# Moving the preparation of the batches from a stage of its own into the rows of the attention stage

## The chip, the cores and the metric

The kernel runs on one core of a Trainium2 chip. The core has five engines with a queue of instructions each: TensorE (PE), VectorE (DVE), ScalarE (ACT), GpSimd (POOL) and SyncE (SP, which here only issues DMAs). They run on their own and wait for each other through semaphores; every engine works its queue strictly in order. The metric is the device time of one execution in microseconds (us); the median of some runs is compared.

## The reference

A block over 16 batches of 512 positions of width 128. The input is normalised; what follows is relative-position attention with 16 heads of 8, a second small attention, and a mixture of experts. The change touches the first two lines and the attention.

```python
xn = layernorm(x)                                   # (16, 512, 128)
q, k, v = xn @ Wq.T + bq, xn @ Wk.T + bk, xn @ Wv.T + bv
idx = clip(pos[None, :] - pos[:, None], -20, 20) + 20
attn = softmax((q @ k.T + einsum("bhqd,qkd->bhqk", q, rel_k[idx])) / sqrt(8))
w = attn @ v + einsum("bhqk,qkd->bhqd", attn, rel_v[idx])
y = x + w @ Wo.T + bo + ffn(xn)
```

## The kernel before, in words

The program is a chain of four stages, each a block of its own between barriers: `prepare`, `attend`, `mix`, `experts`. Names of tiles carry the stage: `p_`, `a_`, `m_`, `e_`; `scr_` is scratch in device memory, through which the stages talk.

**prepare** goes over the 16 batches, two buffers of everything. For batch b it normalises x (statistics on DVE, the power on POOL, the scaling on DVE), transposes it (PE, bank `p_bank_xt`, read by ACT into `p_xnt`), and multiplies it by the three weights (`p_bank_q`, `_k`, `_v`). q, k and k less the left edge (`T[0..2]`, tiles `p_t`) are each split into three bf16 parts, high, middle and low (`p_sp`; the difference that is left is `p_rest`). The relative products (`p_bank_qr`, four query tiles of two halves each, 128x320) are q times the table of relative keys; one half is read by DVE (L201), the other by ACT (L305). POOL takes the products' first column out of them (`qr0`). Everything goes to `scr_parts`, `scr_qr`, `scr_v`, `scr_xn`; `scr_y` gets x + bo. All eight PSUM banks serve this stage.

**attend** goes over the batches again in unrolled rows, one row for a batch, and each row has 16 units u (four query tiles t of four units). A unit computes the scores of four blocks (bank `a_bank_s`, four banks, worked as two pairs):

- PE: scores of pair 0, the transposes of the probabilities of the unit before, j = 0 and 1, scores of pair 1, the products with V of three units before (`attended`, `a_bank_o`), the transposes j = 2 and 3. The scores of a pair may only start when ACT has emptied it in the unit before.
- DVE: for each pair the relative window is added (L815), the negated maximum taken (L846), and one transposed block copied out of the bank (L832, odd j).
- ACT: for each pair one transposed block copied (L899, even j), then two exponentials (L919).

The transposes share **two banks**, `a_bank_pt` 0 and 1. Every user of them is a job in the list `JOBS`, sorted by unit; job n has bank n mod 2, PE does the jobs in this order, and a job may start when the job before it in the same bank has been read. Besides the four `probs` jobs of each unit there are two `features` jobs at the end of every unit with u % 4 = 0 (first one read by ACT, L931, second by DVE, L868) and two `out` jobs at the end of unit 9. After u % 4 = 1 PE does `weigh` and DVE sums and a reciprocal; after u % 4 = 3 DVE does sums.

POOL makes the windows (`a_win`), the features and V with its bias. SP loads everything for the row after: the parts of q, k, kl in 18 DMAs that the list SPREAD hands out over the units (L566), the windows, v and y, and stores the probabilities of each unit.

Of the kernel before, what the change touches and what calls it, by code (L numbers as in the profile page):

```python
# [42 lines left out]
def prepare(nc, x, w, scr, ident_dram):  # L43

    with ExitStack() as ctx:
        def sb(name, shape, dt=F32):  # L50
            return ctx.enter_context(nc.sbuf_tensor("p_" + name, shape, dt))

        def ps(name):
            return ctx.enter_context(nc.psum_tensor("p_bank_" + name, [P, 512], F32))

        def sem(name):
            return ctx.enter_context(nc.semaphore("p_s_" + name))

        ident = sb("ident", [P, P])
        wq, wk, wv = sb("wq", [P, P]), sb("wk", [P, P]), sb("wv", [P, P])  # L60
        qk_bias = sb("qk_bias", [P, 4])
        bias_q = sb("bias_q", [P, 1])
        bias_kl = sb("bias_kl", [P, 1])
        rel = sb("rel", [P, H, FAR + 1])
        relx = sb("relx", [P, H, FAR])
        bo = sb("bo", [P, E])
        X = [sb(f"x{s}", [P, NT, E]) for s in range(2)]
        XN = [sb(f"xn{s}", [P, NT, E]) for s in range(2)]
        Y = [sb(f"y{s}", [P, NT, E]) for s in range(2)]
        stats = sb("stats", [P, NT, 6])  # L70
        mv = sb("mv", [P, NT, 2])
        pows = sb("pows", [P, 2])
        ones = sb("ones", [P, H])
        rstd = sb("rstd", [P, NT])
# [1748 lines left out]
```

## Time and profile before

| | us |
|---|---|
| three runs | 2536.8, 2535.61, 2541.07; median 2536.8 |
| profiled execution, its own time | 2541.16 |
| its span | 2539.2 |
| busy PE, DVE, ACT, POOL | 2166.0, 1971.7, 1574.5, 995.5 |
| first work of `attend` | 239.16 |
| first scores of `attend` | 284.35 |
| last exponential of `attend` ends about | 1624 |

The views list, for a stretch, a line or an instruction: how long an engine was busy, and how long it sat idle before an instruction and what ended that wait. A busy engine waits for nobody, an idle one shows who is late.

### The profile page before, as it was taken

How to read it: one execution, taken by the hardware profiler on the slowest of the kernel's cores; microseconds unless marked ns; L12 is line 12 of the kernel's file. 1: busy time of each engine (PE TensorE's matmuls, PEld its weight loads, DVE VectorE, ACT ScalarE, POOL GpSimd, SP SyncE). 2: the span in 40 equal slices, each digit the busy share in tenths (PEclk: the TensorE clock that was granted, in tenths of full speed). 3: DMA queues.
4: the chain of work that ended last, by engine and by line, in shares of the span. 5: the costliest groups of instructions: out<-in, count | busy, mean ns of one | idle time of the engine just before them, and what ended most of it. 6: DMA issues, size and time to landing. Idle time of an engine off the chain costs nothing. (4 is left out here: it accounts for less than half of the span.)

```text
span 2539.2 us, 78048 instructions
## 1 busy us (share of the span) xinstructions
PE 2166.0 (85%) x27816; PEld 1483.5 (58%) x27816; DVE 1971.7 (78%) x4345; ACT 1574.5 (62%) x3954; POOL 995.5 (39%) x1318
## 2 busy tenths in 40 slices
PE   5673488888888888888888888789999996999999
PEld 3442366666666666666666666546666554666665
DVE  5664399898989889888999999646776765787777
ACT  4442378787877777777878787546777662232222
POOL 5664245445554555455545554300000003333332
PEclk9877699999999999999999999879999998999999
DMA  6887255555554555545555554300101011011010
GB/s 192 268 256 224 81 111 123 110 115 111 125 113 110 117 119 113 116 105 124 111 115 118 118 119 88 65 18 26 37 25 37 25 33 60 29 30 32 25 37 17
DMA packets 572137, 241.21 MB, mean 95 GB/s; under 512 B 466374, under 2 KB 535750, under 8 KB 567238
## 3 DMA queue, kind: packets, MB, share of 16 engines
q1 hardware_dynamic: 571846, 237.28, 37.5%
q8 instruction: 189, 3.10, 0.5%
q14 instruction: 102, 0.84, 0.1%
HBM read 133.87 MB, written 103.29 MB: 93 GB/s over the span
## 5 line engine op out<-in xcount | busy, mean ns | idle before, releaser
L919 ACT ACTIVATE a_probs<-a_bank_s,a_neg_max 128x512 f32<-128x512 f32 x1024 | 694.0, 684 | 203.2 <-DVE a_neg_max L846 199.6
L846 DVE TENSOR_REDUCE a_neg_max<-a_bank_s 128x2 f32<-128x1024 f32 x512 | 626.9, 1224 | 55.7 <-DVE a_bank_s L815 1.4
L694 PE MATMUL a_bank_pt<-a_ident,a_probs 128*128 128x128 f32 x4096 | 590.9, 284 | 54.2 <-ACT a_feat_t L931 42.3
L694 PEld LDWEIGHTS a_bank_pt<-a_ident,a_probs 128*128 128x128 f32 x4096 | 443.1, 142 | 193.1 <-issue 68.8
L899 ACT ACTIVATE a_probs_t<-a_bank_pt 128x512 f32<-128x512 f32 x512 | 304.9, 596 | 146.9 <-PE a_bank_pt L694 144.8
L832 DVE COPY a_probs_t<-a_bank_pt 128x512 f32<-128x512 f32 x512 | 349.3, 682 | 27.5 <-PE a_bank_pt L694 22.1
L715 PE MATMUL a_bank_o<-a_probs_t,a_v 128*32 128x128 f32 x8192 | 285.9, 282 | 1.0
L682 PE MATMUL a_bank_s<-a_kl,a_q 48*32 48x204 bf16 (+14 forms) x3840 | 156.2, 273 | 128.7 <-DMA a_kl<-scr_parts 78.9
L1589 ACT ACTIVATE e_gate<-e_bank_g 128x512 f32<-128x512 f32 x144 | 85.9, 597 | 275.8 <-PE e_bank_g L1528 275.8
L715 PEld LDWEIGHTS a_bank_o<-a_probs_t,a_v 128*32 128x32 f32 x8192 | 215.0, 112 | 56.7 <-issue 33.8
L1005 POOL TENSOR_TENSOR a_win<-a_raw,a_band 128x1152 f32<-128x1152 f32 x64 | 168.6, 2634 | 126.8 <-DVE a_neg_max L846 69.6
L815 DVE TENSOR_TENSOR a_bank_s<-a_bank_s,a_win 128x144 f32<-128x144 f32 (+2 forms) x640 | 161.4, 270 | 57.9 <-PE a_bank_s L682 52.7
L1536 PEld LDWEIGHTS e_bank_y<-e_w,e_hid 128*128 128x128 f32 x1152 | 149.5, 192 | 96.6 <-issue 57.0
L1278 DVE TENSOR_REDUCE m_neg_max<-m_bank_s 128x2 f32<-128x1024 f32 x128 | 156.6, 1224 | 61.4 <-PE m_bank_s L1242 54.1
L919 ACT ACTIVATION_READ_ACCUMULATOR a_probs<-a_bank_s,a_neg_max 128x1 f32 x1024 | 203.2, 198 | 0.0
L682 PEld LDWEIGHTS a_bank_s<-a_kl,a_q 48*32 48x32 bf16 x3840 | 63.2, 89 | 219.1 <-issue 203.6
L1375 ACT ACTIVATE m_probs<-m_bank_s,m_neg_max 128x512 f32<-128x512 f32 x256 | 173.3, 682 | 13.4 <-DVE m_neg_max L1278 5.0
L1251 PEld LDWEIGHTS m_bank_pt<-m_ident,m_probs 128*128 128x128 f32 x1024 | 112.5, 143 | 99.7 <-issue 83.4
L1536 PE MATMUL e_bank_y<-e_w,e_hid 128*128 128x128 f32 x1152 | 156.0, 279 | 17.1 <-DVE e_hid L1698 17.1
L682 PE MATMUL a_bank_s<-a_k,a_q 48*32 48x512 bf16 (+15 forms) x4096 | 169.3, 291 | 0.0
L1341 POOL TENSOR_TENSOR m_rms<-m_rms,m_pows 128x4 f32<-128x4 f32 x16 | 16.1, 1007 | 371.3 <-DVE m_rms L1291 371.3
L1613 DVE SCALAR_TENSOR_TENSOR e_y<-e_bank_y,e_comb,e_y 128x128 f32<-128x128 f32 x512 | 143.8, 343 | 12.3
(166 smaller groups left out, 3576.3 us busy)
## 6 DMA issues: line engine op xcount, KB each, us to landing
scr_probs<-a_probs SPq DMA_DIRECT2D x512, 72.0 KB, 2.7
a_raw<-scr_qr SPq DMA_DIRECT2D x256, 96.0 KB
scr_qr<-p_qr SPq DMA_DIRECT2D x64, 320.0 KB, 2.9
a_feat<-scr_probs SPq DMA_DIRECT2D x256, 78.0 KB, 2.4
scr_parts<-p_sp SPq DMA_DIRECT2D x144, 128.0 KB, 2.9
a_left<-scr_probs SPq DMA_DIRECT2D x256, 64.0 KB, 2.4
a_q<-scr_parts SPq DMA_DIRECT2D x32, 192.0 KB
a_k<-scr_parts SPq DMA_DIRECT2D x32, 192.0 KB
```

The source lines that it names most:

```text
L682: ins = nc.tensor.matmul(b_s[g * QBLK:(g + 1) * QBLK, p, a:z], Q[s][par:par + ROWS, half, at:at + QBLK], keys[s][par:par + ROWS, half, a:z ...
L694: ins = nc.tensor.transpose(b_pt[bank_of(job)][:, 0, t * P:(t + 1) * P], probs[(u - 1) % 4][:, j, MAX_REL + t * P:MAX_REL + (t + 1) * P], ...
L715: ins = nc.tensor.matmul(out, V[s][:, V_SLOTS.index((edge, kt)), j, hh * 24:hh * 24 + 32], blocks[:, :, :, kt * P + j * QBLK:kt * P + (j + ...
L815: ins = nc.vector.tensor_tensor(near, near, bass.AP(own.tensor, own.offset, [own.ap[0], [step, n], [1, z - a]]), ALU.add)
L832: nc.vector.tensor_copy(probs_t[(u - 1) // 2 % 2][:, spot(u - 1, PLACES[j]), :], b_pt[bank_of(job)][:, 0, :]).then_inc(pt_ev[bank_of(job)], 1)
L846: nc.vector.tensor_reduce(neg_max[:, 2 * pair:2 * pair + 2], b_s[:, 2 * pair:2 * pair + 2, :], AX.X, ALU.max, negate=True).then_inc(max_ok, 1)
L899: nc.scalar.activation(probs_t[(u - 1) // 2 % 2][:, spot(u - 1, PLACES[j]), :], b_pt[bank_of(job)][:, 0, :], ACT.Copy).then_inc(pt_ev[bank ...
L919: nc.scalar.activation(probs[u % 4][:, j, MAX_REL:MAX_REL + S], b_s[:, j, :], ACT.Exp, bias=neg_max[:, j:j + 1], accum_out=sums[:, t, PLAC ...
L1005: nc.gpsimd.tensor_tensor(win[t % 2][:], over, band[:].rearrange("p (o h c) -> p o h c", o=1, h=1) .to_broadcast([P, NQB, NJ, WIN]), ALU.m ...
L1278: nc.vector.tensor_reduce(neg_max[:, 2 * pair:2 * pair + 2], b_s[:, 2 * pair:2 * pair + 2, :], AX.X, ALU.max, negate=True).then_inc(max_ok, 1)
L1375: nc.scalar.activation(probs[:, j, :], b_s[:, j, :], ACT.Exp, bias=neg_max[:, j:j + 1], accum_out=sums[s][:, u, j:j + 1]).then_inc(exp_ok, 1)
L1536: ins = nc.tensor.matmul(b_y[k][:, t * P:(t + 1) * P], hid[k][:, t * P:(t + 1) * P], w2[:, e, :], start=True, stop=True)
```

## The change

The stage `prepare` is gone; `attend` holds its work. Row b of the attention prepares batch b + 2 (LEAD = 2). Batch 0 is prepared ahead of everything, and batch 1 in a new row −1 (`lead`), which holds no attention. Rows 0 to 13 hold both kinds of work, rows 14 and 15 attention alone.

- The prepared batch's banks are 12 more jobs in the two banks `a_bank_pt`: the transposed x at the end of unit 3, q at 5, k at 6, v at 13, and two halves of a relative product at each of 10, 11, 14 and 15.
- ACT alone reads the relative products, 128x320 each, and with it takes their first column by an activation of 8 elements (`a_qr_first`), which POOL did. It also makes all the high and middle parts. DVE keeps the statistics (unit 0) and the reading of q (unit 5). POOL normalises x, and makes all differences and low parts.
- Each product of a relative half contracts over the 64 rows that hold its heads, not 128.
- k less the left edge is made from k in SBUF, no longer from the bank.
- v goes from the bank to the tile that POOL reads, without `scr_v`. x + bo is made by POOL in the row that ends the batch, from x loaded there, without the first pass through `scr_y`.
- SP has 19 issues more in a row with preparation (x, xn, nine parts, four of qr, four of the first columns), one less for v; the loads of q, k, kl begin at unit 3.

```diff
-def prepare(nc, x, w, scr, ident_dram):
...
+LEAD = 2
...
+PREP = [(3, "xt", 0), (5, "q", 0), (6, "k", 0), (13, "v", 0)] + [(u, "qr", n) for u in (10, 11, 14, 15) for n in range(2)]
+JOBS += PREP
 JOBS.sort(key=lambda job: job[0])
...
-        SPREAD = [1, 1, 2, 1, 1, 1, 2, 0, 1, 1, 2, 1, 2, 1, 1, 0]
+        SPREAD = [0, 0, 0, 2, 1, 1, 2, 2, 1, 1, 2, 1, 2, 2, 1, 0]
...
+            row(-1, 1, -1, lead=True)
             row(0, 0, 0, first=True)
...
+            for u in range(UNITS):
+                prep(-LEAD, u)
+            prep_rest(0)
+            sp.wait_ge(out_qr, 16 * NT)
+            sp.wait_ge(out_0, 16 * NQB)
+            sp.wait_ge(out_sp, PART_STORES)
             load_left(0, 0)
             load_win(0, 0)
             load_qk(0, 0, STACK)
...
+                    bank_free(pe, b, job)
+                    if job[1] == "xt":
+                        pe.wait_ge(xn_ok, n + 1)
+                        for t in range(NT):
+                            ins = nc.tensor.transpose(bank[:, t * P:(t + 1) * P], X[:, t, :], ident[:])
+                    elif job[1] in ("q", "k"):
+                        job_read(pe, b, (3, "xt", 0))
+                        ins = nc.tensor.matmul(bank, (wq if job[1] == "q" else wk)[:], XNT[:], start=True, stop=True)
...
+                        rows_of = slice(hf * HALF, hf * HALF + HALF)
+                        ins = nc.tensor.matmul(bank[:, 0:G * FAR], T[0][rows_of, t * P:(t + 1) * P],
+                                               relx[rows_of, hf::2, :], start=True, stop=True)
...
+            def read_qr(b, u, t):
+                n = b + LEAD
+                for hf in range(2):
+                    job = (u, "qr", hf)
+                    bank = b_pt[bank_of(job)][:, 0, 0:G * FAR].rearrange("p (h r) -> p h r", r=FAR)
+                    job_done(act, b, job)
+                    need(act, out_qr, n, 16 * NT, 16 * 2 * (t // 2))
+                    need(act, out_0, n, 16 * NQB, 0)
+                    nc.scalar.activation(QR0[:, t, hf::2], bank[:, :, 0], ACT.Copy)
+                    nc.scalar.activation(QR[t % 2][:, hf::2, :], bank, ACT.Copy).then_inc(pt_ev[bank_of(job)], 1)
...
+                if u == 6:
+                    job = (6, "k", 0)
+                    job_done(act, b, job)
+                    need(act, lo_ok[1], n, 1, 0)
+                    nc.scalar.activation(T[1][:], b_pt[bank_of(job)][:, 0, :], ACT.Identity, bias=qk_bias[:, 1:2]
+                                         ).then_inc(pt_ev[bank_of(job)], 1)
+                    job_read(act, b, (5, "q", 0))
+                    high(n, 0)
+                if u == 7:
+                    job_read(act, b, (6, "k", 0))
+                    high(n, 1)
+                    need(act, lo_ok[2], n, 1, 0)
+                    nc.scalar.activation(T[2][:], T[1][:], ACT.Identity, bias=left_less[:]).then_inc(t2_ok, 1)
+                if u == 9:
+                    act.wait_ge(t2_ok, n + 1)
+                    high(n, 2)
+                if u in (10, 11, 14, 15):
+                    read_qr(b, u, (10, 11, 14, 15).index(u))
+                if u in (12, 13, 14):
+                    middle(n, u - 12)
...
+                    if t == 0:
+                        prep(b, 0)
+                    if t == 1 and not first:
+                        g.wait_ge(y_ld, b * 16)
+                        nc.gpsimd.tensor_tensor(y_in[:], y_in[:], bo[:].rearrange("p (o e) -> p o e", o=1)
+                                                .to_broadcast([P, NT, E]), ALU.add).then_inc(bo_ok, 1)
...
-    prepare(nc, a["x"], a, scr, a["ident"])
     attend(nc, a, scr)
```

PE's queue around the end of unit 10 of row 0, before (L715 `attended`, L694 the transposes, L682 the scores):

```order
L715 MATMUL a_bank_o<-a_probs_t,a_v 32x128 x16
L694 MATMUL a_bank_pt<-a_ident,a_probs 128x128 x8
L682 MATMUL a_bank_s<-a_kl,a_q 32x236 x4
L682 MATMUL a_bank_s<-a_kl,a_q 32x300 x4
L682 MATMUL a_bank_s<-a_k,a_q 32x276 x4
L682 MATMUL a_bank_s<-a_k,a_q 32x212 x4
```

and in the changed program (L500, L479 and L467 are the same three, L449 the relative products):

```order
L500 MATMUL a_bank_o<-a_probs_t,a_v 32x128 x16
L479 MATMUL a_bank_pt<-a_ident,a_probs 128x128 x8
L449 MATMUL a_bank_pt<-a_relx,a_t 128x320 x2
L467 MATMUL a_bank_s<-a_kl,a_q 32x236 x4
L467 MATMUL a_bank_s<-a_kl,a_q 32x300 x4
L467 MATMUL a_bank_s<-a_k,a_q 32x276 x4
L467 MATMUL a_bank_s<-a_k,a_q 32x212 x4
```

Two products stand between the last transposes of the unit and the first scores of the next.

ACT's queue over the same unit and the start of the next, before (L899 the copy of a transposed block, L919 the exponentials):

```order
L899 ACTIVATE a_probs_t<-a_bank_pt 128x512
L919 ACTIVATE a_probs,a_sums<-a_bank_s,a_neg_max 128x512 x2
L899 ACTIVATE a_probs_t<-a_bank_pt 128x512
L919 ACTIVATE a_probs,a_sums<-a_bank_s,a_neg_max 128x512 x2
L899 ACTIVATE a_probs_t<-a_bank_pt 128x512
```

and changed (L790 the copy, L816 the exponentials):

```order
L790 ACTIVATE a_probs_t<-a_bank_pt 128x512
L816 ACTIVATE a_probs,a_sums<-a_bank_s,a_neg_max 128x512 x2
L735 ACTIVATE a_qr_first<-a_bank_pt 128x8
L736 ACTIVATE a_qr<-a_bank_pt 128x8x40
L735 ACTIVATE a_qr_first<-a_bank_pt 128x8
L736 ACTIVATE a_qr<-a_bank_pt 128x8x40
L790 ACTIVATE a_probs_t<-a_bank_pt 128x512
```

Four activations stand between the last exponential of a unit and the first copy of the next.

SP's queue from the last load for row 0 on, before:

```order
L566 DMA a_kl<-scr_parts 8x4096
L579 DMA a_v_in<-scr_v 128x512
L656 DMA scr_probs<-a_probs 1x64 x2
L588 DMA a_raw<-scr_qr 32x4x192 x4
L574 DMA a_left_of<-scr_qr 32x4x16 x4
```

and changed (L290 is the load of a window):

```order
L272 DMA a_kl<-scr_parts 8x4096
L409 DMA scr_probs<-a_probs 1x64 x2
L412 DMA scr_qr<-a_ident 1x1
L290 DMA a_raw<-scr_qr 32x4x192 x4
L319 DMA scr_xn<-a_x 128x512
L323 DMA scr_parts<-a_sp 128x512 x3
L339 DMA scr_qr<-a_qr 128x640
L250 DMA a_x<-in_x 128x4x128
L339 DMA scr_qr<-a_qr 128x640 x2
L333 DMA scr_parts<-a_sp 128x512 x3
```

The stores of batch 1 now stand behind all the loads of batch 0 and behind the wait for the margins (`margin_out`).

## Rows read from the trace of the kernel before

**Rows 1.** Busy time by engine, the preparing stage and one row of attention; columns as its header.
```profile
core 0: us, PE busy (x) PEld busy (x) DVE busy (x) ACT busy (x) POOL busy (x), PEclk, DMA share, GB/s
0.00:240.00 240.00, 147.32 (x512) 95.26 (x512) 144.04 (x344) 102.23 (x193) 145.53 (x230) 0.85 0.80 241
...
1076.70:1163.00 86.30, 74.85 (x1333) 54.82 (x1332) 75.40 (x153) 65.99 (x168) 42.34 (x63) 0.96 0.50 111
```

**Rows 2.** Timeline, the start of rows' second POOL step: first and fifteenth of 16.
```profile
404.01 1.27 POOL L1045 TENSOR_TENSOR a_o_sb<-a_o_sb,a_moved_t 128x512 f32<-128x512 f32 x1 [5.38 <-DVE a_o_sb L876]
...
1577.52 1.27 POOL L1045 TENSOR_TENSOR a_o_sb<-a_o_sb,a_moved_t 128x512 f32<-128x512 f32 x1 [11.87 <-DVE a_o_sb L876]
```

**Rows 3.** Timeline, batch 0 in `prepare`, then the seam between the stages.
```profile
32.58 2.79 SPq L169 DMA_DIRECT2D scr_qr<-p_qr  x4
...
239.16 0.35 SPq L550 DMA_DIRECT2D a_ident<-in_ident  x1
...
243.49 2.59 SPq L574 DMA_DIRECT2D a_left_of<-scr_qr  x4
...
284.35 0.23 PE L682 MATMUL a_bank_s<-a_kl,a_q 48*32 48x44 bf16 x4 [60.70 <-DMA a_kl<-scr_parts]
```

**Rows 4.** Timeline of ACT, units 10 to 13: first exponential of each, and feature read.
```profile
1010.23 0.69 ACT L919 ACTIVATE a_probs<-a_bank_s,a_neg_max 128x512 f32<-128x512 f32 x1 [0.73 <-DVE a_neg_max L846]
...
1014.53 0.69 ACT L919 ACTIVATE a_probs<-a_bank_s,a_neg_max 128x512 f32<-128x512 f32 x1 [0.21 <-DVE a_neg_max L846]
...
1019.39 0.69 ACT L919 ACTIVATE a_probs<-a_bank_s,a_neg_max 128x512 f32<-128x512 f32 x1 [0.78 <-DVE a_neg_max L846]
...
1022.92 0.59 ACT L931 ACTIVATE a_feat_t<-a_bank_pt 128x512 f32<-128x512 f32 x1
...
1024.26 0.60 ACT L899 ACTIVATE a_probs_t<-a_bank_pt 128x512 f32<-128x512 f32 x1 [0.75 <-PE a_bank_pt L694]
...
1024.84 0.69 ACT L919 ACTIVATE a_probs<-a_bank_s,a_neg_max 128x512 f32<-128x512 f32 x1
```

**Rows 5.** Timeline of PE at the end of unit 8, and DVE's wait in unit 12.
```profile
1022.56 0.29 DVE L868 COPY a_last_t<-a_bank_pt 128x128 f32<-128x128 f32 x1 [0.42 <-PE a_bank_pt L732]
...
1083.31 1.09 PE L694 MATMUL a_bank_pt<-a_ident,a_probs 128*128 128x128 f32 x8
1085.16 0.63 PE L728 MATMUL a_bank_pt<-a_ident,a_feat 128*128 128x128 f32 x4 [0.76 <-ACT a_probs_t L899]
1085.85 0.33 PE L732 MATMUL a_bank_pt<-a_ident,a_feat 128*128 128x128 f32 x1
1086.11 0.32 PE L682 MATMUL a_bank_s<-a_kl,a_q 48*32 48x236 bf16 x8
```

**Rows 6.** Instructions by line in `prepare`: busy us, mean ns, idle before.
```profile
L285 POOL TENSOR_TENSOR p_sp<-p_rest,p_sp 128x512 bf16<-128x512 f32 x32 | 43.3, 1370 | 0.1
L273 POOL TENSOR_TENSOR p_rest<-p_t,p_sp 128x512 f32<-128x512 f32 x32 | 36.2, 1149 | 2.3 <-ACT p_t L314 2.3
...
L305 ACT ACTIVATE p_qr<-p_bank_qr 128x320 f32<-128x320 f32 x64 | 28.0, 438 | 43.3 <-PE p_bank_qr L344 36.8 <-DMA scr_qr<-p_qr 3.5 <-issue 3.0
...
L323 ACT ACTIVATE p_sp<-p_rest 128x512 bf16<-128x512 f32 x32 | 20.2, 632 | 21.4 <-POOL p_rest L273 21.4
...
L211 DVE TENSOR_SCALAR p_t<-p_bank_q,p_bias_q 128x512 f32<-128x512 f32 x16 | 12.0, 750 | 13.0 <-PE p_bank_q L352 13.0
```

**Rows 7.** Timeline, single pieces of `prepare` with PE at full clock.
```profile
204.55 0.87 DVE L216 BATCH_NORM_STATS2 p_stats<-p_x 128x6 f32<-128x128 f32 x4 [3.42 <-DMA p_x<-in_x]
...
205.66 0.37 DVE L227 BATCH_NORM_AGGREGATE p_mv<-p_stats 128x2 f32<-128x6 f32 x4
...
216.82 1.02 PE L354 MATMUL p_bank_k<-p_xnt,p_wk 128*128 128x512 f32 x2
217.67 1.05 PE L357 MATMUL p_bank_v<-p_wv,p_xnt 128*128 128x128 f32 x8
218.56 2.32 PE L344 MATMUL p_bank_qr<-p_relx,p_t 128*128 128x320 f32 x8
```

**Rows 8.** The end of a row: scores by line, timeline, and the stretch after.
```profile
L682 PE MATMUL a_bank_s<-a_kl,a_q 48*32 48x12 bf16 (+3 forms) x3824 | 155.4, 273 | 64.9 <-ACT a_probs L919 44.7 <-DMA a_kl<-scr_parts 18.2
...
1124.03 0.23 PE L682 MATMUL a_bank_s<-a_kl,a_q 48*32 48x44 bf16 x4 [2.42 <-DMA a_kl<-scr_parts]
...
1125.60:1131.00 5.40, 5.28 (x63) 3.84 (x62) 3.42 (x5) 2.98 (x7) 3.00 (x3) 0.56 0.17 36
```

More of the change, by code:

```diff
@@ L411, with of_row, part @@
 OF_ROW_BEFORE += [(9, "out", n) for n in range(2)]
+def of_row(b):
+    def part(job):
+        if job in PREP:
+            return b + LEAD < B
+        return b < B and (b > 0 or job not in OF_ROW_BEFORE) if b >= 0 and job not in OF_ROW_BEFORE else 0 < b <= B
+    return [job for job in JOBS if part(job)]
+OF_ROW = {b: of_row(b) for b in range(-LEAD, B + 1)}
 def jobs_before(b, job, bank=None):
@@ L757, in project, with row @@
                     ins.then_inc(pt_ps, 1)
-            def row(b, s, m, first=False, tail=False):
+            def row(b, s, m, first=False, tail=False, lead=False):
+                if lead:
+                    for u in range(UNITS):
+                        prep(b, u)
+                    pe.wait_ge(const_ok, N_CONST_OK)
+                    return
                 for u in range(10 if tail else UNITS):
@@ L782, in row @@
                         project(b)
+                    prep(b, u)
+            for u in range(UNITS):
+                prep(-LEAD, u)
             rows(pe, row)
@@ L833, in read_probs, with row @@
                                       ).then_inc(pt_ev[bank_of(job)], 1)
-            def row(b, s, m, first=False, tail=False):
+            def row(b, s, m, first=False, tail=False, lead=False):
+                if lead:
+                    for u in range(UNITS):
+                        prep(b, u)
+                    return
                 for u in range(10 if tail else UNITS):
@@ L895, in read_probs @@
+            for u in range(UNITS):
+                prep(-LEAD, u)
             def read_probs(b, u, j):
@@ L900, in read_probs, with row @@
                                      ).then_inc(pt_ev[bank_of(job)], 1)
-            def row(b, s, m, first=False, tail=False):
+            def row(b, s, m, first=False, tail=False, lead=False):
+                if lead:
+                    for u in range(UNITS):
+                        prep(b, u)
+                    act.wait_ge(const_ok, N_CONST_OK)
+                    act.wait_ge(margin_out, 48)
+                    return
                 for u in range(10 if tail else UNITS):
@@ L1014, in make_window, with row @@
                 nc.gpsimd.tensor_tensor(own[:, :, 0:places], own[:, :, 0:places], left_win, ALU.add).then_inc(win_ok, 1)
-            make_window(0, 0, 0)
-            for kt in range(NT):
-                make_v(0, kt, 0)
-            def row(b, s, m, first=False, tail=False):
+            def row(b, s, m, first=False, tail=False, lead=False):
                 last = isinstance(b, int) and b == B - 1
+                if lead:
+                    prep(b, 0)
+                    for kt in range(NT):
+                        make_v(0, kt, 0)
+                    make_window(0, 0, 0)
+                    for step in (2, 3):
+                        prep(b, step)
+                    return
                 if tail:
```

506 lines of the change are left out of this document (199 added, 307 removed).

## The prediction

> **What bounds the kernel now.** I read first the busy time by stretch [rows 1]. While `prepare` runs, no engine is the bound: in 240 us PE, DVE, ACT and POOL are busy for 147, 144, 102 and 146. A row of attention looks quite different: of 86.3 us PE is busy for 74.9, DVE 75.4, ACT 66.0, POOL 42.3. The mean row, from the first to the fifteenth scale step with 14 rows between them, is (1577.52 − 404.01)/14 = 83.8 us [rows 2]. So 16 batches' preparation costs 240 us by itself, and attention has little left in each of three engines, but POOL half its time.
>
> Second the timeline at the seam [rows 3]. The first batch's last stores are issued at 32.6 us, and `attend` starts at 239.2, but its first scores are at 284.35: from 243.49 on, 40.9 us go into loading batch 0. This wait has nothing to do with preparation and stays.
>
> Third, what sets the pace of a unit [rows 4]. The first exponentials of units 10 and 11 are 4.30 us apart. ACT's waits in front of them end with DVE's maximum, so DVE sets the pace; each pair waits only 0.2 us. From unit 12 to 13, a unit with two `features` jobs, it is 5.45, which is 1.15 more. How two jobs at the end of a unit cost that, PE shows [rows 5]: the last transposes end at 1084.4, PE may not start the first job until ACT has read that bank (0.76 us of waiting), the second until DVE has read the other, and the next scores start at 1086.11, 1.7 us after the transposes. DVE waits 0.42 for its job and then has its own reads. ACT's read costs nothing there, since its next copy waits 0.75 for PE anyway [rows 4]. The added jobs are of this same kind, so this unit is my scale.
>
> **The front, gained.** The sum is made against the profiled execution's 2541.2 us (span 2539.2, and 2.0 around it), which is 4.4 above the median of the runs shown.
>
> Batch 0 must still be prepared before anything is loaded. In `prepare` its stores ended at 32.6 + 2.8 = 35.4 us [rows 3]. Now DVE first prepares the attention's constants, for which it waits for nine more loads (about 4 us, at the spacing of the loads at the seam, 239.16 to 243.49 for nine issues [rows 3]); ACT makes six instead of four high and middle parts and reads all halves, with only two banks; POOL makes three low parts and not two (1.37 more [rows 6]). I take 46 us until all is landed. Then 40.9 for the same loads: 87. Batch 1's arithmetic lies under these loads, but its stores stand behind them on SP, behind the wait for the margins, and ACT's third read of relative products waits until the first two are stored. That is a chain of some seven issues, a landing, and the reads and two products left: I take 11 us. First scores at 98, against 284.35: **186 us gained**. Bounds: 87 if the second batch hides entirely, and 46 + 40.9 + 35.4 = 122 if it runs serially: 162 to 197.
>
> **The rows, lost.** 14 rows hold both. Each engine's added work in a row:
> - PE: eight products of 320 columns. Four of them took 2.32 [rows 7]; contraction over half the rows leaves the columns alone, so 4.64. q and k 1.02 each, v 1.05, the transposed x 0.55 (half of 1.09 [rows 5]). Together 8.3.
> - DVE: statistics 0.87 + 0.37 [rows 7], q 0.75 [rows 6]: 2.0.
> - ACT: eight reads at 0.438, six parts at 0.632 [rows 6], k and kl at the 0.69 of a biased activation, x and v at 0.59 [rows 4], and eight activations of 8 elements, which the trace doesn't show. Through 0.59 at 512 and 0.438 at 320 a line runs to 0.18 at 8; between nothing and 0.44 it is nearest to that. Together 3.5 + 3.8 + 1.4 + 1.2 + 1.4 = 11.3.
> - POOL: three differences, three low parts (1.15 and 1.37 [rows 6]), four passes over 128x512 (1.27 each [rows 2]), less its first columns: about 14. It has 44 idle of 86 [rows 1] and the added steps have whole units before somebody wants them: nothing on the path.
>
> The Trainium skill, "ScalarE: Activation LUTs", section "What ACT_TABLE_LOAD costs", gives 186 ns plus 0.833 ns per element for an activation without a pointer, 93 ns of it overlapped when they run back to back. By this estimate the small read is 0.19 and adds 0.1 to the queue, and ACT's sum would be about 0.6 lower. The trace agrees for the 320 elements (0.438 against 0.453); no row shows the 8.
>
> Now by unit, with the scale above. **Units 10, 11, 14, 15**: behind the transposes PE waits 0.76, does 0.58, waits for DVE's copy, does 0.58, so the scores start about 2.05 after the transposes and DVE adds its window 1.5 later than in a plain unit. ACT's four reads (1.2) run under this, because its next exponentials depend on DVE. In 11 and 15 DVE has sums of 0.5 us there anyway, which the unit spacing from 11 to 12 (4.86 against 4.30 [rows 4]) shows, so 1.0. **Unit 0**: statistics 1.2, in full on DVE. **Unit 3**: wait and 0.55 on PE, half under DVE's sums: 0.4. **Unit 5**: q behind `weigh` 1.0, then DVE's read, part of it hidden: 1.5. **Unit 6**: k 1.02 behind a wait, under DVE's addition: 0.7. **Unit 7**: 1.2 on ACT against its slack of 0.2 a pair and DVE's sums: 0.4. **Unit 13**: v 1.0. **Units 9 and 12**: ACT's part lies in a wait for PE that is there already (the 0.75 [rows 4]): 0. Sum: 1.5 + 1.0 + 1.5 + 1.2 + 0.4 + 1.5 + 0.7 + 0.4 + 1.0 = 9.2 without unit 15. In unit 15 the 1.0 falls together with the wait for the last load of kl, 18.2 us in 15 rows, 1.2 each [rows 8], which is issued at unit 14 and doesn't move: 0.
>
> **9.2 a row, 14 rows: 129 us.** Bounds: 5, if only the statistics, q, and half of the rest show, and 21.6, if all that is added on the three engines stands one behind the other. DMA carries 192 of its 240 us as busy share in `prepare`, 12 a row, and has half its time free [rows 1]; SP's 18 more issues at 0.45 are 8 us of a queue that waits for ACT once a unit. Both hidden; if SP's cover is gone, the kl load is late, which is a rival below. POOL's addition of bo in the tail has PE's projection beside it: 0.3.
>
> Sum: 2541.2 − 186 + 129 + 0.3 = 2484; the runs of before lie 4 lower than the profiled one, so **2480 us**.
>
> **Rivals.** Break-even is 186/14 = 13.3 us a row.
> (a) *ACT becomes the bound; slower.* If its reads do not lie under PE's waits, its 11.3 and DVE's 2.0 show in full, just 13.3. Every `qr` pair frees both banks only when ACT has come through its exponentials, and the next transposes wait for the banks; where DVE's copy waits for them too, PE's 8.3 adds a third. With 16.5 a row: 231, and 2582. For it: ACT has 20 idle us in a row, in pieces of 0.2. Against: the `features` unit has the same form and cost 1.15. The point from which it decides is whether ACT's next copy after a `qr` unit starts later than DVE's maximum is ready. 9%.
> (b) *PE's clock.* After the wait of 2.42 the granted clock was 0.56 in the next stretch, half its instructions at 1.2 GHz [rows 8], and that row took 86.3 instead of 83.8 [rows 1, 2]. If the new waits bring 1.5 such falls a row, 3.8 more: 13.0 a row and 2533. Against: the added jobs make PE busier, the waits are under 1 us. 5%. The Trainium skill, "TensorE: Matmul & The Clock Gate", section "HAM oscillation — how this bites in real kernels", describes this as a matter of waits between groups of matmuls; by that rule this case turns on how long the new waits are, and the trace agrees in that it shows the fall behind the longest wait.
> (c) *SP is late.* Its parts and qr stores stand before the loads of kl; each row waits 2 more at its end: 11.2 a row, 2508. 4%.
> (d) *Better hidden.* 5 a row: 70 us, 2421. Against: three engines are each busy for 76 to 87% of a row. 6%.
> That the change doesn't take the stage away can't be.
>
> **How the numbers follow.** The forecast, a loss of 6.5 to 12 a row, gives 2442 to 2519 and holds 76%. The range reaches up to (b) and (c): 2440 to 2533. About 0.2% (5 us) is what a measurement can tell. Faster: 76 + 6 + 4 and a part of (b), 0.87. Slower: (a) and some of (b), 0.10. Within: 0.03.
>
> **What the profile would show.** First scores near 98 us; after 122 the front was mis-sized. Rows 0 to 13 of 93 us each between scale steps, 14 and 15 as before. In a `qr` unit the exponentials 5.8 apart, ACT's next exponential still waiting for DVE's maximum; if it waits for nothing, (a) holds. DVE's window waiting for PE's scores about 1.4 us there. A granted clock of 0.9 or less in the rows would be (b), a wait for kl over 2 us at each row's start (c). The prediction is wrong above all if the small waits of three in-order queues add up instead of lying under each other.

## The result: a small gain, most of the expected one lost at the ends of the rows

The changed kernel takes 2527.93 us (median of 13 runs, 2517.24 to 2535.47), the kernel before 2539.34 (13 runs, 2535.61 to 2545.2) on the same chip. The ratio is 0.9947, with a 95% interval from 0.9933 to 0.9962: faster by 11 us where 57 were forecast. The profiled execution has a span of 2520.4 us, 18.8 less than that of before.

First the changed kernel's timeline at the places of [rows 2, 3]: the first scores, and the first and fourteenth scale step.

```profile
95.91 0.23 PE L467 MATMUL a_bank_s<-a_kl,a_q 48*32 48x44 bf16 x4
...
226.38 1.27 POOL L991 TENSOR_TENSOR a_o_sb<-a_o_sb,a_moved_t 128x512 f32<-128x512 f32 x1 [11.65 <-DVE a_o_sb L707]
...
1467.27 1.28 POOL L991 TENSOR_TENSOR a_o_sb<-a_o_sb,a_moved_t 128x512 f32<-128x512 f32 x1 [10.76 <-DVE a_o_sb L707]
```

The front is 284.35 − 95.91 = 188.4 us shorter. The 13 rows between the two scale steps take (1467.27 − 226.38)/13 = 95.5 us each, against 83.8. That is 11.6, where 9.2 had been added up.

Now a unit with two `qr` jobs, unit 14 of a row, to compare with [rows 4, 5]. ACT's timeline and one row of DVE's:

```profile
1126.42 0.69 ACT L816 ACTIVATE a_probs<-a_bank_s,a_neg_max 128x512 f32<-128x512 f32 x1 [0.55 <-DVE a_neg_max L677]
...
1129.96 0.18 ACT L735 ACTIVATE a_qr_first<-a_bank_pt 128x8 f32<-128x8 f32 x1
1130.02 0.45 ACT L736 ACTIVATE a_qr<-a_bank_pt 128x320 f32<-128x320 f32 x1
...
1130.46 0.32 DVE L642 TENSOR_TENSOR a_bank_s<-a_bank_s,a_win 128x144 f32<-128x144 f32 x1 [1.28 <-PE a_bank_s L467]
...
1132.14 0.69 ACT L816 ACTIVATE a_probs<-a_bank_s,a_neg_max 128x512 f32<-128x512 f32 x1 [0.28 <-DVE a_neg_max L677]
```

This is what was forecast: exponentials 5.72 apart (5.8), DVE's window waits 1.28 for the scores (1.4), ACT's small read takes 0.18, and ACT still waits for DVE's maximum. (The estimate by the Trainium skill for the small read, 0.19 from "ScalarE: Activation LUTs", section "What ACT_TABLE_LOAD costs", agrees with this 0.18.)

The end of a row looks different. PE's timeline at the last transposes of one row and the first scores of the next, to compare with the wait of 2.42 in [rows 8], and windows behind it:

```profile
1132.89 1.09 PE L479 MATMUL a_bank_pt<-a_ident,a_probs 128*128 128x128 f32 x8
1134.23 1.52 PE L449 MATMUL a_bank_pt<-a_relx,a_t 64*128 64x320 f32 x4 [0.25 <-ACT a_probs_t L790]
1141.61 0.22 PE L467 MATMUL a_bank_s<-a_kl,a_q 48*32 48x44 bf16 x4 [5.86 <-DMA a_kl<-scr_parts]
```

```profile
core 0: us, PE busy (x) PEld busy (x) DVE busy (x) ACT busy (x) POOL busy (x), PEclk, DMA share, GB/s
...
1135.75:1141.60 5.85, 0.00 (x0) 0.02 (x1) 0.00 (x0) 0.82 (x5) 1.24 (x2) 0.77 0.71 222
1141.60:1146.60 5.00, 4.99 (x72) 3.55 (x73) 3.74 (x6) 2.05 (x5) 4.57 (x3) 0.59 0.10 27
1146.60:1151.60 5.00, 4.03 (x79) 2.89 (x77) 3.76 (x15) 3.02 (x7) 1.18 (x2) 1.00 0.22 43
```

For 5.86 us PE and DVE do nothing while the DMA engines carry 222 GB/s, and in the 5 us behind the wait the granted clock is 0.59, most of the stretch at 1.2 GHz; then it is 1.00 again. This is the worst row. The page's group of the scores, and the view of the waits (us in total, times, longest), give the sum: 45.9 us in 15 row starts, against 18.2 in [rows 8].

```profile
L467 PE MATMUL a_bank_s<-a_kl,a_q 48*32 48x204 bf16 (+14 forms) x3840 | 156.4, 275 | 65.3 <-DMA a_kl<-scr_parts 45.9
```

```profile
PE a_bank_s L467 <- DMA a_kl<-scr_parts: 45.9, 15, 5.9
```

The time from the first exponential of a unit to that of the next, as a mean over rows 1 to 13, read from ACT's timeline of each kernel, puts the loss in its place. The last columns anticipate two experiments (e5, e1_again), in which none of these rows waits for kl. Units 2, 4, 8 and 12, forecast at 0, differ by less than 0.2 and stand only in the sum.

| unit | forecast | before | after | added | e5 | e1_again | added, no wait for kl |
|---|---|---|---|---|---|---|---|
| 0 | 1.2 | 5.89 | 7.63 | 1.74 | 5.45 | 6.61 | 1.16 |
| 1 | 0 | 5.42 | 5.06 | −0.36 | 5.47 | 5.00 | −0.47 |
| 3 | 0.4 | 4.71 | 5.08 | 0.37 | 4.71 | 5.11 | 0.40 |
| 5 | 1.5 | 5.76 | 6.52 | 0.76 | 5.41 | 6.54 | 1.13 |
| 6 | 0.7 | 4.90 | 5.22 | 0.32 | 4.90 | 5.23 | 0.33 |
| 7 | 0.4 | 4.86 | 5.11 | 0.25 | 4.86 | 5.11 | 0.25 |
| 9 | 0 | 6.47 | 7.21 | 0.74 | 6.47 | 6.81 | 0.34 |
| 10 | 1.5 | 4.33 | 5.66 | 1.33 | 4.33 | 5.67 | 1.34 |
| 11 | 1.0 | 4.87 | 6.15 | 1.28 | 4.87 | 6.16 | 1.29 |
| 13 | 1.0 | 5.65 | 6.32 | 0.67 | 5.42 | 6.32 | 0.90 |
| 14 | 1.5 | 4.34 | 5.72 | 1.38 | 4.34 | 5.72 | 1.38 |
| 15 | 0 | 5.91 | 9.18 | 3.27 | 4.95 | 5.92 | 0.97 |
| row (all 16) | 9.2 | 83.86 | 95.50 | 11.64 | 81.93 | 90.87 | 8.94 |

Unit 15, costed at 0, takes 3.27: more than the whole excess over the forecast, since the other units together stay 0.8 below it. The theory after reading this was that the last load of kl comes late, and for a reason that the prediction's rival (c) names in part. SP's timeline around that row's end shows where the load stands:

```profile
1127.49 3.14 SPq L308 DMA_DIRECT2D a_feat<-scr_probs  x4
1130.67 1.39 SPq L272 DMA_DIRECT2D a_kl<-scr_parts  x2
1132.11 0.92 SPq L391 DMA_DIRECT2D scr_probs<-a_probs  x2
1133.16 1.99 SPq L290 DMA_DIRECT2D a_raw<-scr_qr  x4
1135.19 1.00 SPq L272 DMA_DIRECT2D a_kl<-scr_parts  x1
```

The last load is issued at 1135.19, when PE is in its last products, and the data lands 5.4 us behind the end of the issue. Behind the feature loads, at unit 13, stand two loads of kl, and then come the windows' four. Before there was one load at unit 13. This is the line `SPREAD` of the diff: its entry for unit 13 went from 1 to 2. The loads come in sizes of 192, 128 and 64 KB, and the last three are one of each in this order, so at unit 13 it is 320 KB now and was 128.

### The profile page after: what moved, and what is told of

It reads as the page before. It is cut to its first block and busy times, and to the rows that moved or that the text cites. A ratio compares the mean times of both kernels' runs of the same rounds, so it can differ in the third digit from the quotient of the medians.

```text
span 2520.4 us, 77225 instructions
## 1 busy us (share of the span) xinstructions
PE 2192.5 (87%) x27816; PEld 1473.3 (58%) x27816; DVE 1866.2 (74%) x4151; ACT 1614.9 (64%) x4178; POOL 1032.2 (41%) x1270
## 5 line engine op out<-in xcount | busy, mean ns | idle before, releaser
L816 ACT ACTIVATE a_probs<-a_bank_s,a_neg_max 128x512 f32<-128x512 f32 x1024 | 694.9, 685 | 131.9 <-DVE a_neg_max L677 128.2
L479 PE MATMUL a_bank_pt<-a_ident,a_probs 128*128 128x128 f32 x4096 | 597.9, 288 | 63.3 <-ACT a_feat_t L828 41.6
L479 PEld LDWEIGHTS a_bank_pt<-a_ident,a_probs 128*128 128x128 f32 x4096 | 452.3, 144 | 201.4 <-issue 74.5
L790 ACT ACTIVATE a_probs_t<-a_bank_pt 128x512 f32<-128x512 f32 x512 | 306.3, 598 | 204.0 <-PE a_bank_pt L479 202.9
L500 PE MATMUL a_bank_o<-a_probs_t,a_v 128*32 128x128 f32 x8192 | 294.5, 287 | 1.2 <-issue 0.2
L500 PEld LDWEIGHTS a_bank_o<-a_probs_t,a_v 128*32 128x32 f32 x8192 | 221.4, 115 | 61.8 <-issue 42.1
L467 PE MATMUL a_bank_s<-a_kl,a_q 48*32 48x204 bf16 (+14 forms) x3840 | 156.4, 275 | 65.3 <-DMA a_kl<-scr_parts 45.9
L816 ACT ACTIVATION_READ_ACCUMULATOR a_probs<-a_bank_s,a_neg_max 128x1 f32 x1024 | 203.8, 199 | 0.0
L467 PE MATMUL a_bank_s<-a_k,a_q 48*32 48x512 bf16 (+15 forms) x4096 | 171.1, 299 | 0.0
L1287 POOL TENSOR_TENSOR m_rms<-m_rms,m_pows 128x4 f32<-128x4 f32 x16 | 16.1, 1008 | 372.9 <-DVE m_rms L1237 372.9
L467 PEld LDWEIGHTS a_bank_s<-a_kl,a_q 48*32 48x32 bf16 x3840 | 59.5, 89 | 186.4 <-issue 172.7
L449 PE MATMUL a_bank_pt<-a_relx,a_t 64*128 64x320 f32 x256 | 101.3, 510 | 62.0 <-ACT a_qr L736 36.5
```

The lines of the kernel that those rows point to most:

```text
L467: ins = nc.tensor.matmul(b_s[g * QBLK:(g + 1) * QBLK, p, a:z], Q[s][par:par + ROWS, half, at:at + QBLK], keys[s][par:par + ROWS, half, a:z ...
L479: ins = nc.tensor.transpose(b_pt[bank_of(job)][:, 0, t * P:(t + 1) * P], probs[(u - 1) % 4][:, j, MAX_REL + t * P:MAX_REL + (t + 1) * P], ...
L500: ins = nc.tensor.matmul(out, V[s][:, V_SLOTS.index((edge, kt)), j, hh * 24:hh * 24 + 32], blocks[:, :, :, kt * P + j * QBLK:kt * P + (j + ...
L790: nc.scalar.activation(probs_t[(u - 1) // 2 % 2][:, spot(u - 1, PLACES[j]), :], b_pt[bank_of(job)][:, 0, :], ACT.Copy).then_inc(pt_ev[bank ...
L816: nc.scalar.activation(probs[u % 4][:, j, MAX_REL:MAX_REL + S], b_s[:, j, :], ACT.Exp, bias=neg_max[:, j:j + 1], accum_out=sums[:, t, PLAC ...
```

## The experiments

All ratios are to the kernel before, run beside it on the same chip. The kernel before takes 2537.23 us on one of the chips and 2546.06 on another, so two experiments on different chips are compared here by their ratios. "Wait for kl" is the sum over the row starts 1 to 15 in the profiled execution.

**e1_kl_early.** All loads issued by unit 12.

```diff
-SPREAD = [0, 0, 0, 2, 1, 1, 2, 2, 1, 1, 2, 1, 2, 2, 1, 0]
+SPREAD = [0, 0, 0, 2, 2, 1, 2, 2, 2, 2, 2, 1, 2, 0, 0, 0]
```

> The changed kernel with its 18 loads of the next row's operands all issued by unit 12 (four more of them between units 4 and 10, none at 13 and 14). Theory (the last load of kl is issued too late and lands after PE has run out of work, 45.9 us of waits in 15 row starts, with a lower clock behind each): the waits for kl fall below 5 us in all, and the time falls by 40 to 50 us, to about 2482. Rival (the wait only hides another lateness at the end of a row, of DVE's maximum or of unit 15's reads of relative products): the waits for kl go, another one takes their place, and less than 15 us are gained. Second rival (the queue is full, so that earlier loads push the loads for the features and the windows back): waits of POOL for the left columns and of PE for kl shift into the row, 2528 or slower.

Measured: 2446.35 us, ratio 0.9643 (0.9617 to 0.9668). No wait for kl is left. Against the changed kernel 77 us are gained by the ratios (0.9947 − 0.9643), well over the 40 to 50 of the theory. The page's group of the scores, and SP's and PE's timelines at a row's end:

```profile
L467 PE MATMUL a_bank_s<-a_kl,a_q 48*32 48x204 bf16 (+14 forms) x3840 | 155.2, 273 | 20.3 <-ACT a_probs L816 20.2
```

```profile
988.14 1.18 SPq L272 DMA_DIRECT2D a_kl<-scr_parts  x2
...
996.50 2.09 SPq L308 DMA_DIRECT2D a_feat<-scr_probs  x4
998.64 1.00 SPq L391 DMA_DIRECT2D scr_probs<-a_probs  x2
999.76 2.89 SPq L290 DMA_DIRECT2D a_raw<-scr_qr  x4
```

```profile
1002.20 1.52 PE L449 MATMUL a_bank_pt<-a_relx,a_t 64*128 64x320 f32 x4 [0.25 <-ACT a_probs_t L790]
1003.65 0.20 PE L467 MATMUL a_bank_s<-a_kl,a_q 48*32 48x44 bf16 x4
```

The scores start as soon as the products are out. Rows 1 to 13 fall from 95.50 to 90.82 us: unit 15 by 3.26, unit 0 by 1.02, unit 9 by 0.39. The waiting itself was 3.06 a row start (45.9/15), so each microsecond of it had cost 1.5 on the mean. Unit 0 is where the clock was low behind the wait: it takes 6.6 in each of these rows in e1, at a granted clock of 1.00, and 7.36 to 8.75 in 11 of the 13 in the changed kernel. That price doesn't follow the length of the wait: 7.66 behind the 5.86, 8.75 behind a wait of 3.39. Row 14, which has no preparation, also falls, from 89.5 to 83.3, because its load of kl was late by the same list. (POOL now waits longer for the left columns, 160.8 us in all against 58.4, and the time falls all the same.)

Unit 9 gains by the clock too. In the changed kernel it takes 6.51 in seven of the 13 rows, with the clock at 1.00, and 8.02 to 8.06 in the other six, with 0.83 or 0.84; in e1 it is long in three rows. Unit 11 takes 5.83, and in three rows of each kernel 7.19 to 7.25. No wait for kl is near. PE's timeline in unit 10 of row 5 and of row 6 of the changed kernel, and windows over both:

```profile
627.37 1.58 PE L449 MATMUL a_bank_pt<-a_relx,a_t 64*128 64x320 f32 x4 [0.54 <-ACT a_probs_t L790]
...
629.42 1.09 PE L479 MATMUL a_bank_pt<-a_ident,a_probs 128*128 128x128 f32 x8
```

```profile
721.69 1.09 PE L479 MATMUL a_bank_pt<-a_ident,a_probs 128*128 128x128 f32 x8
723.33 1.58 PE L449 MATMUL a_bank_pt<-a_relx,a_t 64*128 64x320 f32 x4 [0.55 <-ACT a_probs_t L790]
724.84 0.32 PE L467 MATMUL a_bank_s<-a_kl,a_q 48*32 48x236 bf16 x8
...
725.39 1.54 PE L479 MATMUL a_bank_pt<-a_ident,a_probs 128*128 128x128 f32 x8
```

```profile
629.40:631.80 2.40, 2.38 (x57) 1.81 (x57) 2.30 (x4) 1.72 (x6) 2.40 (x3) 1.00 0.59 153
...
725.40:729.20 3.80, 3.80 (x56) 2.65 (x56) 3.59 (x5) 2.38 (x7) 3.39 (x4) 0.56 0.66 170
```

Both rows do the same work with the same waits, and only in the second does the clock then fall to 1.2 GHz, which makes its unit 11 longer by 1.4; in unit 9 it is 1.5. What decides isn't known. Such falls inside a row are nine in rows 1 to 13 of the changed kernel (1.0 us a row), five in the kernel before (in units 5 and 13, 0.6 a row), six in e1 and in e1_again (0.7), and none in the profile of e5.

**e4_before_spread.** The list alone, in the kernel before.

```diff
-SPREAD = [1, 1, 2, 1, 1, 1, 2, 0, 1, 1, 2, 1, 2, 1, 1, 0]
+SPREAD = [0, 0, 0, 2, 1, 1, 2, 2, 1, 1, 2, 1, 2, 2, 1, 0]
```

> The kernel before with one number list alone from the changed one: the spread of the 18 loads over the units, which begins at unit 3 instead of 0 and has two loads at unit 13 instead of one. Nothing of the preparation moves. Theory (part of the late kl is this list: row 14 of the changed kernel, which stores no parts, still waits 5.7 us for kl): the waits for kl rise from 18.2 to 35 or more in 15 rows and the time by 15 to 25 us, to about 2555 to 2565. Rival (the list is harmless, the added stores and loads alone are at fault): within 4 us of the kernel before.

Measured: 2623.77 us, ratio 1.035 (1.0317 to 1.0383). One list of numbers costs 87 us in a kernel in which nothing else is changed, four times what was expected; the wait for kl is 87.6 us, 69 more than before, so here a microsecond of waiting cost 1.25. SP's and PE's timeline:

```profile
1076.14 1.43 SPq L566 DMA_DIRECT2D a_kl<-scr_parts  x2
1077.62 0.92 SPq L643 DMA_DIRECT2D scr_probs<-a_probs  x2
1078.66 3.07 SPq L588 DMA_DIRECT2D a_raw<-scr_qr  x4
1081.77 0.34 SPq L566 DMA_DIRECT2D a_kl<-scr_parts  x1
...
1087.06 0.23 PE L682 MATMUL a_bank_s<-a_kl,a_q 48*32 48x44 bf16 x4 [5.29 <-DMA a_kl<-scr_parts]
```

**e11_before_one and e10_one_moved.** The list starts at unit 3 as in the change, but unit 13 has one load again; in the kernel before (e11) and in the changed one (e10).

```diff
-SPREAD = [0, 0, 0, 2, 1, 1, 2, 2, 1, 1, 2, 1, 2, 2, 1, 0]
+SPREAD = [0, 0, 0, 2, 2, 1, 2, 2, 1, 1, 2, 1, 2, 1, 1, 0]
```

> The kernel before with the list of e10: it begins at unit 3 as in e4 but has one load at unit 13 as the kernel before. Theory (of the 87 us that e4's list cost, the second load at unit 13 is most): waits for kl of 20 to 40 us in 15 rows and 2540 to 2560. Rival (the late start of the list is what costs, a denser queue all along): waits above 60 us and above 2585.

> The changed kernel with one load of 192 KB moved from unit 13 to unit 12's place in the order (one more at unit 4, one less at unit 13); the last load stays at unit 14, behind the window's four. Theory (the two loads at unit 13, 320 KB in front of the window's 384 KB, make the last one late and slow): waits for kl fall from 45.9 to 15 to 28 us in 15 rows, time 2480 to 2505. Rival (what counts is only whether the last load stands at unit 14 behind the window's loads, in the presence of the preparation's stores): waits of 38 us or more, within 10 us of 2528.

Measured: e11 2547.14 us, ratio 1.0034 (1.0018 to 1.0049), wait 25.5; e10 2485.09 us, ratio 0.9782 (0.9757 to 0.9807). Both as the theory had it. The late start of the list costs 0.3%; the second load at unit 13 costs, by the ratios, the other 80 us in the kernel before and 42 in the changed one. From the view of the waits of e10:

```profile
PE a_bank_s L467 <- DMA a_kl<-scr_parts: 18.3, 9, 3.2
```

This is, to 0.1 us, the 18.2 of the kernel before; that the sums agree so closely is partly chance, since it is 9 row starts here and was 11. e10 is so the kernel that the prediction had in mind, with a wait for kl that "doesn't move": it was forecast at 2480 and takes 2485; its rows are 92.58 − 83.86 = 8.7 longer than before, against 9.2.

**e8_one_at_13.** The last load at unit 13, in front of the windows.

```diff
-SPREAD = [0, 0, 0, 2, 1, 1, 2, 2, 1, 1, 2, 1, 2, 2, 1, 0]
+SPREAD = [0, 0, 0, 2, 2, 1, 2, 2, 2, 1, 2, 1, 2, 1, 0, 0]
```

> The changed kernel with its last load issued at unit 13, none at unit 14: half way between it and e1. Theory (a load is late when it is issued less than 6 us of landing before PE ends the last transposes, which is some 4 us after unit 15's first exponential): at unit 13 it is issued some 5 us before that exponential, just in time; waits for kl below 8 us in all, 2450 to 2460. Rival (the dense queue at units 13 to 14 makes the landing so slow that unit 13 is late too): waits of 15 to 30 us and 2475 to 2500.

Measured: 2455.42 us, ratio 0.9666 (0.9647 to 0.9684), wait 5.4 us in 2 row starts, 5.2 of it in the last one. The theory's result, but not for its reason: the load isn't issued 5 us before unit 15's first exponential, as expected, but 0.8 before, because SP comes late to unit 13 as well. It lands in time all the same: in front of it stand the loads of left columns and features, and not the windows' 384 KB. In the two starts with a wait it landed 2.5 and 2.8 us after its issue. That the missing bytes are the reason is argued from this, not tested.

**e2_small_stores.** Every store of parts and relative products in the rows cut to a 4 by 8 piece; loads of parts and windows read batch 0's or batch 1's. The kernel leaves out the stored values from batch 2 on.

```diff
+def cut(b, whole):
+    return whole if b < 0 else whole[0:4, 0:8]
-sp.dma_start(scr["parts"][n, k, 0], SP[k][0][:]).then_inc(out_sp, 16)
+sp.dma_start(cut(b, scr["parts"][n, k, 0]), cut(b, SP[k][0][:])).then_inc(out_sp, 16)
...
-rows_in = scr["parts"][b, n, part, par * HALF:(par + 1) * HALF]
+rows_in = scr["parts"][min(b, 1), n, part, par * HALF:(par + 1) * HALF]
...
```

> The changed kernel with every store of parts and relative products in a row of attention cut to a 4 by 8 piece; issues and their order stay. Left out: the stored values, so that the rows from the third on read batch 1's parts and windows. This takes some 2.4 MB a row from the DMA engines and nothing from SP's list of instructions. Theory (the load is late because SP stands in waits for landings, and the landing itself is slow, both from the engines' traffic): the last load of kl is issued about 1 us before unit 15's first exponential as in the kernel before, lands in under 5 us instead of 6.3, and the waits for kl fall from 45.9 to 15 to 20; time 2490 to 2505. Rival (SP's added instructions are what delays the load): the waits stay above 35 us, and the time within 8 us of 2528.

Measured: 2478.63 us, ratio 0.9765 (0.9734 to 0.9796), wait 19.4 us. The bytes of the stores do take part: without them the last load is issued 1.7 us earlier, as the theory had it. Its other half failed: the load doesn't land in under 5 us, but in 5.93, as slowly as with the stores. The rival, that SP's added instructions alone are at fault, falls.

These rows of the timelines, taken together over all row starts (the landing only of those where PE waited, counted from the end of the issue), separate two things:

| kernel | KB of kl at unit 13 | issue ended, against unit 15's first exponential | landed behind it | wait for kl, sum | time |
|---|---|---|---|---|---|
| before | 128 | −0.93 | 4.29 (11 starts) | 18.2 | 2539.3 |
| e11 (before) | 128 | −0.35 | 4.23 (13) | 25.5 | 2547.1 |
| e4 (before) | 320 | +2.15 | 5.60 (15) | 87.6 | 2623.8 |
| after | 320 | +0.73 | 5.82 (15) | 45.9 | 2527.9 |
| e2 (stores cut) | 320 | −0.95 | 5.93 (9) | 19.4 | 2478.6 |
| e10 | 128 | +0.09 | 4.50 (9) | 18.3 | 2485.1 |

The landing goes with what stands in front: 4.2 to 4.5 us with 128 KB at unit 13, 5.6 to 5.9 with 320, whether stores are cut or not. e11 against e4, and e10 against the changed kernel, differ in one load's place alone. (Its bytes and its number of packets weren't separated.) The moment of the issue is delayed by both the list and the stores. A part of this is a wait that SP's own view of waits shows: before it reads the left columns it waits until the stored probabilities have landed, 38.6 us in all in the kernel before, 65.0 with the list alone (e4), 79.8 in the changed kernel, and 66.3 with its stores cut (e2). In e10 it is still 79.3, and the issue comes 0.6 earlier: of the 42 us that this load costs, more is the landing, 1.3 a row start, than the issue. The Trainium skill, "DMA: Bandwidth & Descriptors", section "Queues, rings and completion order", says that each DMA engine takes the descriptors of a queue in order and that the increment of the semaphore lands only after every earlier write of that engine; the landings above agree with it.

**e3_qr_shared and e6_early_shared.** DVE reads the second half of each relative product, in the changed kernel and in that of e1.

```diff
 # ScalarE
-for hf in range(2):
+for hf in range(1):
 # VectorE
+job_done(v, b, (u, "qr", 1))
...
+nc.vector.tensor_copy(QR0[:, t, 1::2], bank[:, :, 0])
+nc.vector.tensor_copy(QR[t % 2][:, 1::2, :], bank).then_inc(pt_ev[bank_of(job)], 1)
```

> The changed kernel, but the second half of each relative product (its first columns too) is read by DVE instead of ACT: the part 'ScalarE alone empties the banks' undone. Theory (in units 10, 11, 14 and 15 ACT waits for DVE's maximum and DVE sets the pace): DVE's two reads, some 0.6 us, come on the pace, 4 units in 14 rows of 0.3 to 0.6: 15 to 35 us slower, 2545 to 2560. Rival (ACT's four reads set the pace there): 10 to 30 us faster.

> Loads early as in e1, and the second half of each relative product read by DVE as in e3. With the kl wait gone the sharing is seen by itself. Theory (DVE sets the pace in the qr units, ACT's reads lie under its wait): units 10, 11, 14, 15 are each 0.1 to 0.25 longer than in e1, 6 to 14 us slower than e1. Rival (ACT's reads set the pace): at least 5 us faster than e1.

Measured: e3 2528.94 us, ratio 0.9965 (0.9948 to 0.9983), with a wait for kl of 53.4 us, and an interval that overlaps the changed kernel's; e6 2451.4 us, ratio 0.9631 (0.9618 to 0.9644). Its base, the kernel of e1 again on the same chip:

> The kernel of e1 once more, as the base for the next three on the same chip: 2446, within 5 us.

which took 2451.2 us, ratio 0.9624 (0.9606 to 0.9643). (The 2446, within 5, is missed by 0.2; the kernel before is slower on this chip too, 2546.06.) So the sharing costs less than either theory had: units 10, 11, 14 and 15 differ by +0.12, −0.03, +0.29 and +0.14 from e1_again, and in rows where the clock is 1.00 by 0.09, 0, 0.08 and 0; the time differs by nothing that can be measured. Which engine empties these banks makes no difference that the time shows.

**e7_early_no_first.** Without ACT's reads of 8 elements from batch 1 on.

```diff
-nc.scalar.activation(QR0[:, t, hf::2], bank[:, :, 0], ACT.Copy)
+if n == 0:
+    nc.scalar.activation(QR0[:, t, hf::2], bank[:, :, 0], ACT.Copy)
```

> Loads early as in e1; ACT's eight reads of 8 elements in a row (the first columns of the relative products) are left out from batch 1 on, so that the stored first columns stay batch 0's. It takes 8 x 0.18 = 1.4 us from ACT in a row. Theory (ACT's part of a qr unit is hidden, as the prediction had it): within 5 us of e1. Rival (a): ACT is on the path, and 8 to 20 us are gained.

Measured: 2446.78 us, ratio 0.9613 (0.9597 to 0.9628), 4.4 us under e1_again with intervals that overlap. Units 10, 14 and 15 are the same to 0.01 us, unit 11 is 0.33 shorter. That is the clock and not the reads: unit 11 takes 5.83 in both where the clock is 1.00, and falls to 1.2 GHz behind unit 10 in three rows of e1_again and in none here. ACT's small reads are hidden in all four units.

**e9_early_q_act.** The read of q in unit 5 by ACT.

```diff
-nc.vector.tensor_scalar(T[0][:], b_pt[bank_of(job)][:, 0, :], Q_SCALE, bias_q[:], ALU.mult, ALU.add
...
+nc.scalar.activation(T[0][:], b_pt[bank_of(job)][:, 0, :], ACT.Identity, bias=bias_q[:], scale=Q_SCALE
...
```

> Loads early as in e1; the read of q with scale and bias in unit 5 done by ACT (0.69) instead of DVE (0.75). Theory (DVE sets the pace of a unit and ACT has room): unit 5 is 0.3 to 0.75 shorter, 4 to 10 us faster than e1. Rival (ACT has no room of 0.7 in one piece, its next copy comes late): 0 to 5 us slower.

Measured: 2450.79 us, ratio 0.9623 (0.9607 to 0.964). Inconclusive: unit 5 is 0.28 shorter (6.26), just under what the theory named, and units 3 and 11 are a little longer, by falls of the clock in one and four rows; the time can't be told from e1_again.

**e5_before_early.** The kernel before with its own loads early.

```diff
-SPREAD = [1, 1, 2, 1, 1, 1, 2, 0, 1, 1, 2, 1, 2, 1, 1, 0]
+SPREAD = [1, 1, 2, 1, 1, 1, 2, 1, 1, 2, 2, 1, 2, 0, 0, 0]
```

> The kernel before with its 18 loads all issued by unit 12 (one more each at units 7, 9, none at 13 and 14), nothing else changed. Theory (its own kl wait of 18.2 us in 15 rows, with the clock behind it): the wait goes, and 25 to 32 us with it: 2505 to 2513. Rival (before, the wait only hides DVE's lateness): within 8 us of 2537.

Measured: 2514.09 us, ratio 0.9902 (0.9883 to 0.992), and no wait for kl between rows. The gain of 26 us is the theory's (25 to 32). The old kernel had a loss of 1% at the same place. It also gives the comparison in which no row waits for kl: from e5 to e1_again the change gains 1 − 0.9624/0.9902 = 2.8%, some 70 us, where the terms of the sum gave 57. The two profiled executions differ by 54.3 only; that of e5 is 8.5 below its own median and has no fall of the clock. Its rows cost 8.94 more, so 14 of them 125 us; 129 had been forecast.

## Why the prediction was wrong

**The front was right.** 186 forecast, 188.4 measured. The loads of batch 0 begin at 44.60, where 46 had been taken, and lead 40.2 us later, with 40.9 taken, to the second window's. After the second window's loads at 84.81 the first scores come at 95.91, 11.1 us later; 11 was the estimate.

**The added work was right in sum, with some luck.** In the `qr` unit 10 above the scores start 2.06 after the transposes (724.84 against 721.69 + 1.09), 2.05 forecast. The table's last column has 8.94 for the 9.2, unit by unit within 0.4, but for two: unit 15 shows 0.97, which is the 1.0 that was set to nothing, and unit 1 is 0.47 shorter, for which no cause was looked for. The 1.0 doesn't lie under the wait: in e10, with the old wait, unit 15 is 1.06 longer than before (6.97). Units 5 and 6, each 0.4 under their forecast, and unit 1 make up for it. And 0.7 of the 8.94 are the falls of the clock inside e1_again's rows, so the work itself is some 8.2.

**One step failed: "the wait for the last load of kl ... is issued at unit 14 and doesn't move: 0".** Its unit doesn't move, but what stands in front of it does. The list `SPREAD` stood in the diff with a second load at unit 13, and the prediction took SP's issues as hidden without counting the bytes ahead of the last load. By e10 this step cost 42 us in the changed kernel, where moving one load away from unit 13 restores the old wait, and by e4 and e11 80 in the kernel before. Rival (c) named the place and the sign, "SP is late", gave it 2 us a row and 4%. The waits are (45.9 − 18.2)/15 = 1.8 longer, near its 2, but the rows 95.50 − 92.58 = 2.9. Its reason, the parts and `qr` stores, was half of it: e2, with the stores cut, also gains 46 us. So the load was late from both together, and taking away either is enough to come back to the old wait. What (c)'s price left out is the clock behind the longer waits, which (b) described.

**Rival (b) was true in a small part.** Falls do come inside the changed kernel's rows, in the features unit 8 and in the `qr` unit 10, behind waits under 1 us, which (b)'s "against" took as safe. But they are nine in 13 rows where the kernel before has five, each costs 1.4 to 1.5 and not 2.5, and in units 5 and 13, where q and v now keep PE busy, the changed kernel has none. The difference is 0.4 a row. Over rows 1 to 13 the granted clock is 0.96, before 0.98, and not the 0.9 that would have been (b).

**The books.** The profiled executions differ by 18.8 us, the forecast had 57. Rows 1 to 13 cost 2.4 us each more than forecast (32 us); row 14, which was to be as before, took 6.2 more and what lies behind it 4.4; row 0 cost 1.5 less, and the front gained 2.4 more. 32 + 6.2 + 4.4 − 1.5 − 2.4 = 38.7, where 57 − 18.8 = 38.2 are to be explained; the rest is rounding.

**The other rivals.** (a), ACT as the bound, is not so: ACT waits for DVE's maximum in the `qr` units, and e7 and e6 find nothing in ACT's reads that the time shows. (d), 5 a row, is not so either, by the 8.94.

**Slips in the prediction's working.** None moves the sum. POOL's terms add up to 12.6 at most and not to 14. The line through 0.59 and 0.438 gives 0.19 at 8 elements, not 0.18; 0.18 was measured. 13.3 and a third of 8.3 are 16.1 a row for (a), not 16.5, and so 2576. And a granted clock of 0.56, between the levels 0.5 and 1.00, is nine tenths of a stretch at 1.2 GHz, not half.

**Left open.** In e4 the last load is issued 1.4 us later than in the changed kernel with the same list and more stores; why was not separated. That the wait is so much longer in e4 comes only in part from this: the changed kernel's `qr` products keep PE busy for longer behind unit 15's first exponential and cover some of it.

**The better version.** The changed kernel with e1's list takes 0.9643 of the kernel before, 0.9624 when measured again, and so 3.1% less than the changed kernel (0.9643/0.9947). None of the complete kernels is measurably faster.

## What to carry to other kernels

A table that says in which slot each transfer is issued is part of the change, also when the slot of the critical one stays: count the bytes and the waits in front of the last transfer that a stage needs, and compare its landing with the moment when the engine runs dry. Test such a list by itself, in the old kernel too; here it alone was worth −1% to +3.5%. And cost a wait at a stage's boundary with what follows it: here each microsecond was worth 1.25 in e4 and 1.5 in the changed kernel, since the clock falls behind the longer waits, at a price that doesn't grow with them.

## What was not expected of the hardware

- 192 KB more in front of a load of 64 KB made it land 1.3 to 1.4 us later (4.2 to 4.5 against 5.6 to 5.9 us).
- A wait of 5.86 us on PE left a granted clock of 0.59 for the 5 us behind it. The waits of 3.06 a row start came with 1.02 us of loss in the unit behind them, and the single losses don't go by the length of the wait.
- The granted clock also fell to 1.2 GHz behind a wait of 0.55 us, and didn't in the row before with the same work and a wait of 0.54. Nine such falls in 13 rows cost 1.4 to 1.5 us each.
- An activation of 8 elements took 0.18 us between others.
